# A new order of the preface and the first body in a graph attention kernel, with edge operations up to four units ahead

## The reference

```python
h = jnp.maximum(_layernorm(x, axis=-1), 0.0)
Wh = h @ W
e = (Wh @ a1)[:, None] + (Wh @ a2)[None, :]
e = jax.nn.leaky_relu(e, negative_slope=ALPHA)
scores = jnp.where(adj > 0, e, jnp.float32(NEG_INF))
attention = jax.nn.softmax(scores, axis=1)
h_prime = attention @ Wh
return x + jax.nn.elu(h_prime)
```

## Time and profile before

| | us |
|---|---|
| median of 3 runs (lowest to highest) | 693.64 (692.67 to 693.67) |
| the profiled execution's own time | 694.66 |
| its span | 692.8 |
| busy: TensorE, VectorE, ScalarE | 632.5, 621.0, 631.4 |
| busy: GpSimd | 53.4 |
| moved by DMA | 275.15 MB, mean 397 GB/s |
| of it in SP's queue (x and adjacency) | 270.67 MB |

### The profile page before, as it was taken

The page is one execution under the profiler, slowest core; times in us unless marked ns, Lnnn a source line. Parts: engine busy times, 40 slices in busy tenths (PEclk is TensorE's granted clock), DMA queues, the critical chain, the costliest instruction groups (busy, mean ns, idle before and its releaser), DMA issues.

```text
span 692.8 us, 23845 instructions
## 1 busy us (share of the span) xinstructions
PE 632.5 (91%) x10422; PEld 621.6 (90%) x10422; DVE 621.0 (90%) x625; ACT 631.4 (91%) x366; POOL 53.4 (8%) x51
## 2 busy tenths in 40 slices
PE   4867999999998989989898998989898998989895
PEld 4747999999998989989898998989898998989895
DVE  5898979999999899898989899898989989898983
ACT  4797999999999989989898998989899898989881
POOL 5000001011000101010010101001010100001010
PEclk9987999999999999999999999999999999999998
DMA  9876899999999999999999999999999999999960
GB/s 323 360 292 260 347 374 386 422 429 425 428 425 430 427 427 429 424 430 425 429 424 429 428 427 425 427 429 425 429 427 426 428 426 429 424 429 427 427 293 19
DMA packets 24840, 275.15 MB, mean 397 GB/s; under 512 B 3088, under 2 KB 7440, under 8 KB 8432
## 3 DMA queue, kind: packets, MB, share of 16 engines
q1 hardware_dynamic: 22864, 270.67, 93.3%
q0 software_dynamic: 1488, 4.07, 1.5%
q10 hardware_dynamic: 464, 0.07, 0.1%
HBM read 272.70 MB, written 2.10 MB: 397 GB/s over the span
## 4 chain that ended last, share of the span: by engine, by line
DMA 32%; DVE 29%; ACT 22%; issue 11%; PE 5%; DVEq 1%; ACTq 1%; SPq 0%
DMA adj_ring<-in_adj 31%; DVE code L651 18%; ACT work L513 16%; DVE work L664 4%; ACT work L521 4%; DVE code L658 1%; PE psum L876 1%; PE psum L896 1%; PE psum L894 1%; PE psum L827 1%; DMA Wx<-in_L_gnn_W 1%; PE psum L817 1%; DVE last_steps L682 1%; DVE last_steps L686 1%; ACT trow L496 1%
## 5 line engine op out<-in xcount | busy, mean ns | idle before, releaser
L896 PE MATMUL psum<-V,work 128*128 128x130 f16 x4096 | 495.3, 221 | 0.0
L894 PE MATMUL psum<-V,work 128*128 128x130 f16 x4096 | 495.0, 220 | 0.0
L513 ACT ACTIVATE work<-trow,Wh 128x4096 int8<-128x4096 f32 x128 | 476.8, 3725 | 0.0
L894 PEld LDWEIGHTS psum<-V,work 128*128 128x128 fp8e4 x4096 | 403.1, 98 | 0.0
L896 PEld LDWEIGHTS psum<-V,work 128*128 128x128 fp8e4 x4096 | 398.7, 97 | 0.0
L651 DVE TENSOR_SCALAR code<-adj_ring 128x4096 uint8<-128x4096 int32 x128 | 293.3, 2292 | 32.7 <-DMA adj_ring<-in_adj 32.7
L876 PE MATMUL psum<-identb,code 128*128 128x128 bf16 x2048 | 137.0, 220 | 41.7 <-DVE code L658 41.6
L658 DVE SCALAR_TENSOR_TENSOR code<-work,code 128x1024 int32<-128x1024 int32 x128 | 156.8, 1225 | 7.9 <-ACT work L513 4.0
L876 PEld LDWEIGHTS psum<-identb,code 128*128 128x128 bf16 x2048 | 119.8, 98 | 48.0 <-DVE code L658 30.8
L521 ACT COPY work<-psum 128x1024 int32<-128x1024 int32 x128 | 129.8, 1014 | 35.9 <-PE psum L876 35.9
L664 DVE TENSOR_SCALAR work<-work 128x1024 int32<-128x1024 int32 x128 | 87.9, 686 | 1.7 <-ACT work L521 1.7
(11 more groups left out here) (76 smaller groups left out, 151.3 us busy)
## 6 DMA issues: line engine op xcount, KB each, us to landing
adj_ring<-in_adj SPq DMA_DIRECT2D x128, 2048.0 KB, 16.9
work<-in_x SPq DMA_DIRECT2D x4, 512.0 KB, 6.0
last_steps<-in_x POOLq DMA_DIRECT2D x16, 128.0 KB, 6.6
out_y<-last_steps POOLq DMA_DIRECT2D x15, 128.0 KB, 7.8
out_y<-last_steps SPq DMA_DIRECT2D x1, 128.0 KB, 1.9
W<-in_L_gnn_W ACTq DMA_DIRECT2D x2, 16.0 KB, 5.4
Wx<-in_L_gnn_W ACTq DMA_DIRECT2D x2, 16.0 KB, 5.6
a_sb<-in_L_gnn_a ACTq DMA_DIRECT2D x1, 0.5 KB, 3.9
```

The lines of the kernel that those rows point to most:

```text
L513: nc.scalar.activation(sign[:, k % 2].bitcast(I8), trow[:, h * UW:(h + 1) * UW], ACT.Sign, bias=(Wh[:, B, 0:1] if isinstance(B, int) else ...
L894: nc.tensor.matmul(sums_of[:, 0:FP], up8[:, j // 2, j % 2], V[:, jb, 0:FP], start=h == 0 and j == 0, stop=False, skip_group_check=True)
L896: last = nc.tensor.matmul(sums_of[:, FP:2 * FP], down8[:, j // 2, j % 2], V[:, jb, FP:2 * FP], start=False, stop=h == 1 and j == HB - 1, s ...
```

## The change

All four compute engines' programs ahead of body 1 are written in a new order; the body loop is changed on VectorE only. No operation, tile or size is changed.

- VectorE: edge operations 0 to 3 go between the copies of Wh and the extrema, operations 4 to 11 between products, low parts and codes. When body 1 begins, 12 edge operations are done instead of 10.
- VectorE's loop: edge operations four units ahead in bodies 1 to 5. Body 6 leaves out those at k = 0 and 1, and from there on they stand two ahead, as before.
- ScalarE: spreads 0 to 3 and sign passes 0 and 1 come ahead of `uu`, which waits for the limits; the high parts come later, between copies and passes. Waits for codes are written out where the new order needs them.
- TensorE: the transposes of x no longer wait for W; `t_round` 0 to 3 come ahead of the extrema; the total stands behind the transposes of units 0 and 1 instead of ahead of both; the first body's transposes and multiplications are interleaved differently. W's second pair of loads counts on a semaphore of its own.

Cut to its core (rows with only "..." stand for what is left out):

```diff
                 copy_Wh(0)
-                variance(2)
+                edges(0, 0)
                 copy_Wh(1)
                 variance(3)
+                edges(0, 1)
                 copy_Wh(2)
+                edges(0, 2)
                 copy_Wh(3)
...
+                codes(0, 0)
                 dve.wait_ge(s_extp, 2)
                 nc.vector.tensor_copy(lim[:, 0:4], psum[:, 7, P:P + 4]).then_inc(s_lim, 1)
+                edges(0, 3)
...
+
+                FAR, NEAR, CHANGE = 4, 2, 6
+
+                def body(i, lead, start=0, last=False):
                     for k in range(BU):
                         if not (last and k + 1 >= BU):
                             codes(i, k + 1)
                         find_ups(i, k)
-                        if k == 1 and not first:
+                        if k == 1:
                             take_sums(i - 1, 1)
                             divide(i - 1)
-                        if k == 4 and not first:
+                        if k == 4:
                             result(i - 1)
                         if k == 7:
                             take_sums(i, 0)
-                        if k + lead < (BU if last else BU + 2):
+                        if k >= start and not (last and k + lead >= BU):
                             edges(i, k + lead)
...
-                body(0, first=True)
-                with dve.Fori(1, NI - 1) as i:
-                    body(i)
-                body(NI - 1, last=True)
+
+                with dve.Fori(1, CHANGE) as i:
+                    body(i, FAR)
+                body(CHANGE, NEAR, start=FAR - NEAR)
+                with dve.Fori(CHANGE + 1, NI - 1) as i:
+                    body(i, NEAR)
+                body(NI - 1, NEAR, last=True)
...
+                spread(1)
                 deviation(3)
+                spread(2)
                 act.wait_ge(s_norm, 2)
                 nc.scalar.activation(ext[0:F, 2:3], norm2[:, :], ACT.Sqrt, scale=float(F)).then_inc(s_sq2, 1)
 
                 nc.scalar.activation(unused[:, 1:2], ones[:, 0:1], ACT.Exp).then_inc(s_table, 1)
-                spread(1)
-
+                spread(3)
+                act.wait_ge(s_trow, 4)
+                act.wait_ge(s_var, 3)
+                step(0, 0)
+                act.wait_ge(s_var, 4)
+                step(0, 1)
                 act.wait_ge(s_lim, 1)
                 t_all = Wh[:, :, 1]
...
                 def t_round(r):
 
+                    pe.wait_ge(s_Whc, r + 1 if t_bank[r] < 4 else 2 * NR - 1)
+                    pe.wait_ge(s_hTc, NR)
                     before = [q for q in range(r) if t_bank[q] == t_bank[r]]
                     if before:
                         pe.wait_ge(s_trow, before[-1] + 1)
...
+                t_round(6)
+                t_round(7)
+                pe.wait_ge(s_trow, 8)
+                transpose_unit(0, 1)
+                for g in range(JB // TR):
+                    last = nc.tensor.matmul(total_ps.rearrange("p (r f) -> p r f", f=F), ones[:, :],
+                                            Wh[:, g * TR:(g + 1) * TR, 3:FX], start=g == 0, stop=g == JB // TR - 1)
+                last.then_inc(s_total, 1)
+                transpose_unit(0, 2)
+                pe.wait_ge(s_trow, JB // TR)
+                multiply_unit(0, 0, first=True)
+                transpose_unit(0, 3)
+                transpose_unit(0, 4)
```

More of the change, by code:

```diff
@@ L589, in _, with body @@
                     .then_inc(s_umin, 1)
-                act.wait_ge(s_trow, JB // TR)
-                def body(i, first=False, last=False):
+                act.wait_ge(s_code, TWO + 7)
+                step(0, 8)
+                copy_unit(0, 6)
+                copy_lows(0, 0)
+                copy_unit(0, 7)
+                act.wait_ge(s_code, TWO + 8)
+                step(0, 9)
+                copy_unit(0, 8)
+                act.wait_ge(s_code, TWO + 9)
+                step(0, 10)
+                def body(i, last=False):
                     for k in range(BU):
@@ L595, in body @@
                             copy_unit(i, k + 1)
-                        if k == 0 and not first:
+                        if k == 0:
                             copy_lows(i - 1, 1)
@@ L746, in _ @@
                 nc.vector.reciprocal(lim[:, 5:6], lim[:, 4:5]).then_inc(s_lim, 1)
-                edges(0, 0)
+                codes(0, 1)
                 dve.wait_ge(s_lim, 3)
@@ L751, in _ @@
                 products(0)
-                edges(0, 1)
+                edges(0, 4)
+                codes(0, 2)
+                products(1)
                 low_parts(0)
-                codes(0, 0)
-                products(1)
-                edges(0, 2)
+                find_ups(0, 0)
+                edges(0, 5)
                 low_parts(1)
+                codes(0, 3)
+                find_ups(0, 1)
+                products(2)
                 dve.wait_ge(s_total, 1)
@@ L760, in _ @@
                     .then_inc(s_acc[1], ONE)
+                dve.wait_ge(s_lim, 1)
                 nc.vector.tensor_scalar(yy[:, :], Wh[:, :, 0], lim[:, 0:1], 0.0, ALU.add, ALU.min).then_inc(s_yy, 1)
-                def body(i, first=False, last=False):
-                    lead = 3 if first else 2
+                codes(0, 4)
+                products(3)
+                edges(0, 6)
+                find_ups(0, 2)
+                low_parts(2)
+                edges(0, 7)
+                find_ups(0, 3)
+                codes(0, 5)
+                low_parts(3)
+                find_ups(0, 4)
+                edges(0, 8)
+                find_ups(0, 5)
+                codes(0, 6)
+                edges(0, 9)
+                edges(0, 10)
+                codes(0, 7)
+                codes(0, 8)
+                find_ups(0, 6)
+                take_sums(0, 0)
+                find_ups(0, 7)
+                edges(0, 11)
+                dve.wait_ge(s_umin, 1)
+                nc.vector.tensor_scalar(flag[:, :], umin[:, :], lim[:, 5:6], LEAST * SPLIT, ALU.mult,
+                                        ALU.is_lt).then_inc(s_flag, 1)
+                dve.wait_ge(s_ab, 1)
+                FAR, NEAR, CHANGE = 4, 2, 6
+                def body(i, lead, start=0, last=False):
                     for k in range(BU):
@@ L898, in multiply_unit @@
                     last.then_inc(s_mult, 1)
-                def body(i, first=False, last=False):
+                transpose_round(0)
+                pe.wait_ge(s_w, 32)
+                nc.tensor.transpose(psum[0:F, 7, 0:P], W2[:, :], ident[:, :]).then_inc(s_wp, 1)
+                transpose_round(1)
+                pe.wait_ge(s_wt, 1)
+                pe.wait_ge(s_aext, 2)
+                nc.tensor.matmul(psum[:, 7, P:P + 3], WT[:, :], a_ext[:, :], start=True, stop=True).then_inc(s_wp, 1)
@@ L901, in body @@
+                multiply_unit(0, 5, first=True)
+                transpose_unit(0, 7)
+                transpose_unit(0, 8)
+                multiply_unit(0, 6, first=True)
+                multiply_unit(0, 7, first=True)
+                def body(i, last=False):
                     for k in range(BU):
```

150 lines of the change are left out of this document (70 added, 80 removed).

## The result

The median fell from 693.65 to 682.77 us (four runs of each; the changed kernel from 681.88 to 683.51), a ratio of 0.9845 with a 95% interval of 0.9829 to 0.9861. That is 10.9 us. The profiled execution has a span of 680.8 us.

The account below looks back on a forecast made before the run. The transfer queue bounds the steady part, ScalarE the start. Of 22.2 us missing queue time, 6.5 and 4.1 stay lost, so 11.6 us are won: 693.64 - 11.6 = 682.0 us, range 676.5 to 689.5.

Parts of the forecast that it names:

- The regimes: Whole kernel before: ScalarE's sign passes set the pace early, transfers at 427 GB/s in the steady part.
- the missing queue time: From 20 to 120 us: shortfalls below 427 GB/s, together 22.2 us of queue time, the ceiling of the gain.
- The sum over VectorE: Preface and first body: VectorE's operation times added up, edge operation 6 ending at 62.4 us and 8 at 76.3.
- the 6.5 and 4.1 us of the sum: First body: queue time still lost at tile 10 (6.5 us) and tile 12 (4.1 us), waiting for edge operations 6 and 8.
- more is won: Rival, start of the kernel: both queue losses turn out small, 16 to 22 us won, 671.4 to 678; chance 0.07.
- The lead of four: Bodies 1 to 5: edge operations four ahead release tile 16's slot in time; two ahead it comes 8.5 us late.
- The debt: From body 1: the 8.5 us lateness, made up at 0.31 us a unit, gone after 27 units.
- The trailing by 9.4 us: Once the queue is the bound: engines four units behind instead of two, 9.4 us, made up over the remaining 76 units.
- The rival on TensorE's clock: From 45 us: pauses leave TensorE at its low clock, gain eaten after about 36 us, 712 us at worst; chance 0.06.
- The larger loss of 14 us: First body: queue loss if ScalarE again stands 3.52 us before its copy, leaving 8 us won.
- the rival of the lead at 690.5 us: Bodies 1 to 5: the lead buys nothing, only 3.1 us won, 690.5 us; chance 0.20.
- One of the signs named: From 20 to 120 us: no stretch of 20 us under 330 GB/s if the forecast is right.

Follow-up runs that it names:

- e5: The changed kernel with edge operation 6 ahead of products(3) and edge operation 8 ahead of low_parts(3): 682.56 us, ratio 0.9831.
- e12: The changed kernel with unit 2's transposes ahead of the total, edge operations 6, 8, 9 and, in bodies 1 to 5, that of k = 1 sooner: 681.89 us.
- e11: The changed kernel with edge operations 6 and 8 sooner as in e5 and the extra TensorE transposes of e10: 681.77 us, ratio 0.9819.
- e1: The changed kernel with edge operations two ahead instead of four from body 1 on, changed preface kept: 690.02 us, ratio 0.9947.
- e9: The changed kernel, unaltered, run again as the measure for runs beside it: 682.19 us, ratio 0.9829.
- e3: The changed kernel with the switch from four to two ahead in body 3 instead of 6: 684.84 us, ratio 0.9863.
- e4: The changed kernel with edge operations four ahead in all bodies: 691.95 us, ratio 0.9972.
- e7: The changed kernel with 24 and 30 extra transposes, read by nobody, in TensorE's two pauses: 681.48 us, ratio 0.9811.
- e10: The same kernel as e7, run again beside the unaltered changed kernel: 680.89 us, ratio 0.9805.

## Why the prediction was right, step by step

- **The regimes** were read rightly. What decides is how many bytes the queue moves before it is the bound: the missing queue time fell from 22.2 to 10.7 us, and the time by 10.9.
- **The sum over VectorE** gave 62.4 and 76.3 us for the ends of edge operations 6 and 8. They ended at 60.46 + 2.20 = 62.7 and 74.28 + 2.20 = 76.5. The sum came out, 10.6 us said and 10.7 measured, but with some luck. The queue runs dry twice, as said, and the two stops were each a little shorter than the 6.5 and 4.1 us of the sum:

```profile
58.00:66.00 8.00, 8.00 (x142) 8.00 (x140) 8.00 (x8) 4.99 (x4) 0.00 (x0) 1.00 0.37 129
...
74.00:80.00 6.00, 5.24 (x89) 4.97 (x87) 5.74 (x5) 4.44 (x5) 2.64 (x1) 1.00 0.53 186
```

  Against 427 GB/s that is 5.6 and 3.4 us. The other 1.7 us are spread over the rest of the stretches, up to 140 us, and the sum had no term for them.
- **What these losses mean** was wrong. I treated them as the cause of what is left. e5 released both slots sooner and gained nothing that can be measured, since the queue then waits at tiles 13 and after; e12 gained no more. By the sum's own figures two limits are of one size: the early losses, and the time from which ScalarE's passes plus four slots let the queue run. e11, which was to lift both, did not lift the second, so this is argued and not shown. The step held this figure in hand, "ends at 95.0: just in time" against a need at 95.9, and should have concluded that no gain beyond the sum was to be had; the rival "more is won" deserved less than it was given.
- **The lead of four** was sized at 8.5 us, and e1 measures 7.1 (8.2 against e9). Two ahead, the sum had edge operation 12 start at 102.1 us; in e1 it starts at 100.96. The debt was said to be gone by body four or five; e3 found about 2 us left after two bodies instead of 3.5. That is what 16 units at the prediction's 0.31 us leave of 7.1, so it fits the rate, and by it the debt would be gone after 23 units instead of 27, half a body sooner. The trailing by 9.4 us that must be made up measured 8.8 (e4), and it was made up.
- **The rival on TensorE's clock** had the start of its condition, 0.50 from 40 to 50 us, but not for long: it is at 0.99 from 50 us on, once the total has begun. In e9, the same kernel, it is 0.99 from 40 to 45 us and 0.67 from 45 to 50, and the total takes 8.00 us instead of 8.81, so the low stretches are not alike in every execution. By e7 and e10 it cost 1 to 2 us, if anything, where a single low stretch of some 4 us was priced at 2. The cover that I named, VectorE as the bound until edge operation 6, did not hold for ScalarE. One reading against this rival was too broad: in the stretch of the kernel before from 20 to 40 us, which was to show that transposes keep the clock at 1.00, 7.12 us are the long total.
- **The ends of the case and the range.** The larger loss of 14 us was tied to ScalarE standing 3.52 us before its copy. It stood 3.01 us and the queue lost 10.7, so that condition did not carry the loss given to it. And the range, said to leave out the larger gain and the slow rival, also left out the rival of the lead at 690.5 us, with 0.20 the likeliest of all: its upper end was 689.5.
- **One of the signs named contradicted the sum**: that no stretch of 20 us would be under 330 GB/s. By my own sum 8.8 of the 10.6 us fall between 60 and 80 us, which leaves 239 GB/s; 256 were measured. Two more were missed narrowly: edge operation 0 ended at 20.1 us and not before 20, and the stretch from 100 to 120 us is at 412 GB/s and not 427.
- **The last edge operation** was said to start near 662 us and started at 660.82; the tail, said to stay at 19.4 us, is 20.0.

## What to carry to other kernels

Where a transfer queue bounds the steady part and an engine bounds the start, the time is set by how much the queue moves before the two change roles: add up the missing GB/s in stretches, and that is the ceiling. Then ask for each loss what the queue would wait for next if it were gone; here removing a loss that the trace showed plainly gained nothing measurable, while 4.3 us on an engine that the averages call covered cost 3 to 4 us. A lead in a ring is worth having while the engines are behind the queue and costs its own length in the tail, so it should end once they have caught up.

## What the runs showed of the hardware

In e7 TensorE did nothing but transposes from 36 to 46 us (busy 9.11 of 10 us, the 54 extra float32 ones among them), and its granted clock stayed at 1.00. In the changed kernel, with pauses of 3.04 and 2.76 us in the same place, it was 0.50 from 40 to 50 us; the total behind took 8.81 us there and 7.17 in e7. Transposes were also all that ran while the clock came back: in the changed kernel it is 0.51 from 33 to 36 us and 1.00 again from 37 to 38, with nothing else on TensorE from 32.01 us on. So transposes did raise the granted clock here, which speaks against the rule of the Trainium skill, TensorE: Matmul & The Clock Gate, "Part 4: PE-mode transpose", that the prediction weighed. The kernel issues them as transposes and the profile lists them as MATMUL; no row shows whether they ran in the mode that the page means.

Of one and the same kernel, two executions had their low stretches in different places (0.50 and 0.50 against 0.99 and 0.67 from 40 to 45 and 45 to 50 us), and what came behind moved by 1.0 us with them. The rate of the queue, 427 GB/s, was the same in every kernel once enough tiles were asked for.
